# Second attention with q computed transposed and the last dense stage in its block: a decoder of four stages on one core

## What is computed

```python
x = x + tanh(g_xattn[0]) * attention0(layernorm(x), ctx)
x = x + tanh(g_ffn[0])   * swiglu(layernorm(x))
x = x + tanh(g_xattn[1]) * attention1(layernorm(x), ctx)
x = x + tanh(g_ffn[1])   * dense1(layernorm(x))

def attention1(latents, context):      # 32 heads, 8 key/value heads, head size 128
    kv = concatenate([context, latents], axis=1)          # 64 + 256 keys
    q = rms_norm((latents @ Wq).reshape(b, n, 32, 128), q_norm_w)
    k = rms_norm((kv @ Wk).reshape(b, m, 8, 128), k_norm_w)
    v = (kv @ Wv).reshape(b, m, 8, 128)
    p = softmax(q @ k.T / sqrt(128))
    return (p @ v) @ Wo

def dense1(x):                         # 1024 tokens
    base, logits = x @ base_W.T, x @ gate_W.T             # 28 experts
    gate_full = scatter of softmax(top2(logits))          # two of 28
    h = (x @ lora_A) * (gate_full * 2)                    # 28 x rank 8
    return base + h @ lora_B
```

## Time and profile before

| | us |
|---|---|
| median of 3 runs | 1496.01 |
| lowest and highest | 1492.74 to 1496.33 |
| profiled execution, its own time | 1493.15 |
| its span in the trace | 1491.4 |
| PE busy | 1399.5 (94%) |
| DVE busy | 1058.6 (71%) |
| ACT busy | 798.0 (54%) |

### The profile page before, as it was taken

One profiled execution on the slowest core, in us unless ns is written; L12 is line 12 of the kernel. 1 busy time (PEld: TensorE's weight loads), 2 busy tenths in 40 slices (PEclk: granted clock), 3 DMA queues, 4 the chain that ended last, 5 costly groups with the idle time before them and its releaser, 6 DMA issues. The chain is left out here.

```text
span 1491.4 us, 24301 instructions
## 1 busy us (share of the span) xinstructions
PE 1399.5 (94%) x7976; PEld 1199.3 (80%) x7976; DVE 1058.6 (71%) x2794; ACT 798.0 (54%) x2204; POOL 462.6 (31%) x588
## 2 busy tenths in 40 slices
PE   4999999998999998999999999999999999999889
PEld 4888888887778876888878888888888878887767
DVE  6777777778633337787787787787787777787765
ACT  4777777775211315565555555555555555555521
POOL 3855555554954612111111121111211111112120
PEclk8999999999999999999999999999999999999989
DMA  4111122111321301001001001001001000100001
GB/s 191 71 55 60 70 70 70 65 61 44 104 68 43 123 1 71 1 1 72 1 1 71 0 1 71 0 1 71 0 1 71 0 36 35 38 18 1 1 0 57
DMA packets 14958, 63.96 MB, mean 43 GB/s; under 512 B 1760, under 2 KB 1760, under 8 KB 10656
## 3 DMA queue, kind: packets, MB, share of 16 engines
q1 hardware_dynamic: 14880, 63.07, 11.8%
HBM read 60.97 MB, written 2.10 MB: 42 GB/s over the span
## 5 line engine op out<-in xcount | busy, mean ns | idle before, releaser
L1251 ACT ACTIVATE p<-psum,nb,rq 128x320 f32<-128x320 f32 x256 | 155.3, 614 | 161.8 <-DVE nb L1034 161.8
L55 PE MATMUL psum<-w1q_hi,xnT_lo 128*128 128x512 f32 x256 | 107.2, 419 | 12.8 <-DVE v_lo L1054 8.3
L964 POOL TENSOR_TENSOR rk<-ssk,rms_eps 128x3 f32<-128x3 f32 x32 | 6.3, 196 | 349.9 <-DVE ssk L1071 349.9
L999 DVE TENSOR_TENSOR pT_lo<-psum,pT_hi 128x512 fp32r<-128x512 f32 x128 | 88.1, 689 | 32.5 <-ACT pT_hi L1174 30.7
L1030 DVE TENSOR_REDUCE mx<-psum 128x2 f32<-128x640 f32 x128 | 105.0, 820 | 5.7
L1215 ACT ACTIVATE q_raw<-psum 128x512 f32<-128x512 f32 x64 | 38.3, 598 | 121.3 <-PE psum L57 121.3
L361 DVE TENSOR_TENSOR VW_lo<-psum,VW_hi 64x512 fp32r<-64x512 f32 x128 | 88.0, 688 | 19.1 <-ACT VW_hi L457 17.5
L57 PE MATMUL psum<-w1q_hi,xnT_hi 128*128 128x512 f32 x256 | 100.6, 393 | 0.0
L55 PE MATMUL psum<-w1o_hi,oT_lo 128*128 128x512 f32 x256 | 100.4, 392 | 0.0
L56 PE MATMUL psum<-w1o_lo,oT_hi 128*128 128x512 f32 x256 | 100.3, 392 | 0.0
L56 PE MATMUL psum<-w1q_lo,xnT_hi 128*128 128x512 f32 x256 | 99.8, 390 | 0.0
(11 more groups left out here) (245 smaller groups left out, 4676.8 us busy)
## 6 DMA issues: line engine op xcount, KB each, us to landing
raw_q<-in_w0q SPq DMA_DIRECT2D x8, 1024.0 KB, 4.8
raw_o<-in_w0o SPq DMA_DIRECT2D x8, 1024.0 KB, 4.8
raw_q<-in_w1q SPq DMA_DIRECT2D x8, 1024.0 KB, 7.5
raw_o<-in_w1o SPq DMA_DIRECT2D x8, 1024.0 KB, 4.8
raw_kv<-in_w_gu SPq DMA_DIRECT2D x10, 512.0 KB, 3.6
raw_gu<-in_w_gu SPq DMA_DIRECT2D x10, 512.0 KB, 3.6
raw_kv<-in_w0kv SPq DMA_DIRECT2D x8, 515.0 KB, 3.3
raw_kv<-in_w1kv SPq DMA_DIRECT2D x8, 512.0 KB, 5.5
```

The source lines that it names most:

```text
L55: pe.matmul(out, w[1], m[0], start=start, stop=False)
L999: last = dve.tensor_tensor(k.pT[1][:, kt, 2 * hp:2 * hp + 2, :], bank.rearrange("p (h q) -> p h q", h=2), f(k.pT[0][:, kt, 2 * hp:2 * hp + ...
L1251: last = act.activation(k.p1[:, tile, h, :], s_pair(j)[:, h % 2, :], ACT.Exp, bias=k.nb[:, i:i + 1], scale=k.rq[:, i:i + 1], accum_out=k.r ...
```

## The change

Attention 1. q is made transposed: the weights are the stationary operand and the normed tokens stream, so that a bank holds two heads x 256 tokens, channels on the partitions. A half is 24 products of 256 columns instead of 12 of 512. ACT makes `qT_hi` from it (`q_hi`), DVE `qT_lo` (`q_lo`), then ACT squares it into `q_sq` (`q_square`). The sum over channels, which now lie on the partitions, is made by PE: eight products with `q_sq` stationary (128x128, plain float32) and a column of ones streaming, each into one column of a bank. DVE adds epsilon and copies it to `ssq`. `q_raw`, its copies, the squares on DVE and the transpositions of q go. `PAIRS` runs by head pair, so that a head pair's rows are complete after two of four scores.

Last dense stage. The block `ffn1_phase` becomes a class whose steps are called from attention 1's `tail`, with the turns and outputs of unit 31 between them. Its weights are split in unit 31 in place of the next g's (`split_next = b == BATCH - 1`), those of `w_b` by POOL, the buffers are views of attention 1's (`w_q`, `qT`, `kT`, `q_sq`, `dump`), and `ag` has one bank instead of two.

```diff
-    PAIRS = [(0, 0), (0, 1), (1, 0), (1, 1)]
+    PAIRS = [(0, 0), (1, 0), (0, 1), (1, 1)]
...
-            def q_squares(n, b, tile):
-                dve.wait_ge(q_copied, 2 * n + tile + 1)
-                for h in range(GH):
...
+            def q_lo(n, b, hp):
+                dve.wait_ge(qt_hi, 2 * n + hp + 1)
+                dve.tensor_tensor(k.qT[1][:, 2 * hp:2 * hp + 2, :],
+                                  y_bank(b, "q", hp)[:, :].rearrange("p (h q) -> p h q", h=2),
+                                  f(k.qT[0][:, 2 * hp:2 * hp + 2, :]), ALU.subtract).then_inc(qt_split, 1)
...
                     if prev:
                         t_lo(n, b, 1)
+                    q_lo(n, b, 0)
                     dve.wait_ge(rk_ready, n + 1)
...
-                    q_squares(n, b, 0)
+                    q_lo(n, b, 1)
                     if prev:
                         t_lo(n, b, 4)
                         t_lo(n, b, 5)
-                    q_squares(n, b, 1)
-                    if prev:
                         pv_lo(n, b, 0)
+                    dve.wait_ge(ssq_full, n + 1)
+                    dve.tensor_scalar(k.ssq[:, :], x_bank(b, "ssq")[:, 0:2 * GH], HD * RMS_EPS, None,
+                                      ALU.add).then_inc(ssq_ready, 1)
                     dve.wait_ge(kt_hi, n + 1)
...
+            def q_hi(n, b, hp):
+                act.wait_ge(q_full, 2 * n + hp + 1)
+                act.activation(k.qT[0][:, 2 * hp:2 * hp + 2, :],
+                               y_bank(b, "q", hp)[:, :].rearrange("p (h q) -> p h q", h=2), ACT.Copy).then_inc(qt_hi, 1)
+
+            def q_square(n, b, hp):
+                act.wait_ge(qt_split, 2 * n + hp + 1)
+                act.activation(k.q_sq[:, hp, :], y_bank(b, "q", hp)[:, :], ACT.Square).then_inc(q_squared, 1)
...
                         if j in (1, 3):
-                            act.wait_ge(q_full, 2 * n + j // 2 + 1)
-                            act.activation(k.q_raw[:, j // 2, :], y_bank(b, "q", j // 2)[:, :], ACT.Copy)\
-                               .then_inc(q_copied, 1)
+                            if j == 3:
+                                q_square(n, b, 0)
+                            q_hi(n, b, j // 2)
+                    q_square(n, b, 1)
+                    if prev:
+                        pv_evac(n, b, 0)
...
-                        for c in range(CH):
-                            if prev and tile == 0 and c == CH - 1:
-                                pe.wait_ge(t_split, 6 * (n - 1) + 1)
-                            last = mm3(pe, y_bank(b, "q", tile)[:, :], [w[:, c, t * PART:(t + 1) * PART] for w in k.xnT],
-                                       [w[:, c, :] for w in k.w_q], c == 0, c == CH - 1)
+                        for hh in range(2):
+                            h = 2 * hp + hh
+                            for c in range(CH):
+                                if prev and hp == 0 and hh == 1 and c == CH - 1:
+                                    pe.wait_ge(t_split, 6 * (n - 1) + 1)
+                                last = mm3(pe, bank[:, hh * SEQ:(hh + 1) * SEQ],
+                                           [w[:, c, h * HD:(h + 1) * HD] for w in k.w_q],
+                                           [w[:, c, b * SEQ:(b + 1) * SEQ] for w in k.xnT], c == 0, c == CH - 1)
...
-                        for h in range(GH):
-                            last = pe.transpose(x_bank(b, "q", tile)[:, h * PART:(h + 1) * PART],
-                                                k.q_raw[:, tile, h * HD:(h + 1) * HD], k.ident[:, :])
+                    pe.wait_ge(q_squared, 2 * n + 2)
+                    for j, (tile, hp) in enumerate(PAIRS):
+                        for hh in range(2):
+                            at = hh * SEQ + tile * PART
+                            last = pe.matmul(x_bank(b, "ssq")[:, 2 * j + hh:2 * j + hh + 1], k.q_sq[:, hp, at:at + PART],
+                                             k.one[:, :], start=True, stop=True)
+                    last.then_inc(ssq_full, 1)
+                    if prev:
+                        p_v(n, b, 1)
...
+                ffn1.pe_ag(pe, 0)
+                turn(n, 0, 0, alone=True)
+                turn(n, 0, 1, alone=True)
+                ffn1.pe_ag(pe, 1)
+                ffn1.pe_base(pe, 0)
+                turn(n, 0, 2, alone=True)
+                turn(n, 0, 3, alone=True)
+                ffn1.pe_base(pe, 1)
+                turn(n, 0, 4, alone=True)
+                turn(n, 0, 5, alone=True)
+                pe.wait_ge(x_added, 2 * (n - 1))
+                p_v(n, 0, 0, alone=True)
+                ffn1.pe_ag(pe, 2)
                 p_v(n, 0, 1, alone=True)
+                ffn1.pe_base(pe, 2)
+                ffn1.pe_hgT(pe, 0)
+                out(n, 0, 0)
+                ffn1.pe_low_rank(pe, 0)
```

More of the change, by code:

```diff
@@ L18 @@
+import math
 import concourse.bass as bass
@@ L930, in piece, with weights @@
         return slice(i * n, (i + 1) * n)
+    def weights(kind, g, i):
+        s = piece(kind, i)
+        if kind == "kv" and isinstance(g, int) and g == NKV:
+            c = slice(2 * i, 2 * i + 2)
+            return k.raw_ag[:, c, :], k.w_ag[0][:, c, 0:LR + NEXP], k.w_ag[1][:, c, 0:LR + NEXP]
+        return raw[kind][:, s], flat[kind][0][:, s], flat[kind][1][:, s]
     def loop(eng, body, tail):
@@ L938, in loop @@
         tail(NKV * BATCH)
+    ffn1 = Ffn1(k, sem, ln, free={"kv": kv_wlo, "q": q_wlo, "exp": exp_done, "scores": s_full, "w_kv": kv_full,
+                                  "turned": t_split, "x": x_added, "whi": kv_whi}, conv=CONV, units=UNITS)
     with nc.Block() as block:
@@ L1105, in body @@
                     last.then_inc(kt_split, 1)
[L1106 to L1113, removed]
+                    if prev:
+                        pv_lo(n, b, 1)
+                    split_next = b == BATCH - 1
                     row_max(n, 0)
@@ L1226, in body @@
                         w_hi("q", g + 1, 0)
-                    for tile in range(2):
-                        act.wait_ge(qt_full, 2 * n + tile + 1)
-                        act.activation(k.qT[0][:, tile, :, :],
-                                       x_bank(b, "q", tile)[:, :].rearrange("p (h q) -> p h q", h=GH),
-                                       ACT.Copy).then_inc(qt_hi, 1)
-                        if prev and tile == 0:
-                            pv_evac(n, b, 1)
-                        if tile == 0:
-                            for late in ln_tiles(n):
-                                ln.act_norm(act, *late)
+                    if prev:
+                        pv_evac(n, b, 1)
+                    for late in ln_tiles(n):
+                        ln.act_norm(act, *late)
                     if split_next:
@@ L1624, in build, with ffn1_views, cut, twice @@
-def build(nc, d, out, phases=("attn0", "ffn0", "attn1", "ffn1")):
+    k.ffn1_load = load
+def ffn1_views(k):
+    k.raw_ag = k.raw_kv[:, 0:CH * (LR + NEXP)].rearrange("p (c n) -> p c n", c=CH)
+    k.w_ag = [w[:, :].rearrange("p (c n) -> p c n", c=CH) for w in k.w_kv]
+    k.w_base = k.w_q
+    k.w_b = [w[:, :, :].rearrange("p (t h) q -> p t (h q)", t=2) for w in k.qT]
+    spare = k.kT[0][:, :, :].rearrange("p b n -> p (b n)")
+    k.hgT = [spare[:, i * 512:(i + 1) * 512].rearrange("p (u c n) -> p u c n", u=2, c=2) for i in range(2)]
+    k.ag, k.hg = k.q_sq[:, :, 0:256], k.q_sq[:, :, 256:256 + LR]
+    small = k.dump[:, :, :].rearrange("p a b -> p (a b)")
+    at = [0]
+    def cut(n, dtype=None):
+        ap = small[:, at[0]:at[0] + n]
+        at[0] += 16 * math.ceil(n / 16)
+        return ap.bitcast(dtype) if dtype else ap
+    def twice(n, dtype=None):
+        return [cut(n, dtype) for _ in range(2)]
+    k.iota_i, k.iota = cut(NEXP, mybir.dt.int32), cut(NEXP)
+    k.top, k.idx, k.idxf = twice(8), twice(8, mybir.dt.uint32), twice(2)
+    k.gap, k.eg, k.pr = twice(1), twice(1), twice(4)
+    k.ga, k.gb, k.gm = twice(NEXP), twice(NEXP), twice(NEXP)
@@ L1626, in build @@
+def build(nc, d, out):
     k = Kernel()
@@ L1686, in build @@
-        done = sem("out_done")
-        with nc.Block() as block:
-            @block.sync
-            def _(sp):
-                sp.dma_start(out.rearrange("(t p) c -> p t c", p=PART), k.x[:, :, :]).then_inc(done, 16)
-                sp.wait_ge(done, 16)
+        with ExitStack() as scope:
+            k.bo, k.gbo = sb(scope, "bo", [HID]), sb(scope, "gbo", [HID])
+            k.w_q, k.w_o = pair(scope, "w0q", [QW]), pair(scope, "w0o", [QW])
+            k.bias, k.q_last = sb(scope, "bias", [GH + 2]), sb(scope, "q_last", [GH])
+            k.kvT = pair(scope, "kvT0", [2, BATCH * CTX])
+            k.WK = pair(scope, "WK", [CH, BATCH, GH, CTX])
+            k.VW = pair(scope, "VW", [GH // 2, BATCH, HID])
+            k.p0 = sb(scope, "p0", [4, GH * CTX])
+            k.nb0, k.sum0 = (sb(scope, n, [2, GH]) for n in ("nb0", "sum0"))
+            k.rinv0 = sb(scope, "rinv0", [4, GH])
+            k.pT0 = pair(scope, "pT0", [2, 2 * PART])
```

(8 more changed lines are left out.)

543 lines of the change are left out of this document (263 added, 280 removed).

## The result

The changed kernel takes 1524.93 us (median of 5 runs, 1523.99 to 1535.39), the kernel before 1494.68 us (5 runs, 1491.33 to 1496.33): ratio 1.022, 95% interval 1.019 to 1.025. It is slower by 30 us. Forecast were 1512 us and a range of 1482 to 1554: the sign and the range hold, the point is 13 us too low.

The account below looks back on a forecast made before the run. PE's instructions and waits were taken to bound attention 1, waits between engines the tail. 1493.15 + 29.8 (PE's work) + 2 (waits) - 14 (tail), plus 1 for timed runs, gave 1512 us; range 1482 to 1554, own range 1497 to 1525.

Parts of the forecast that it names:

- The products: Eight one-column float32 products per unit on PE in attention 1, two weight loads each: +1.74 us a unit.
- The first rival: A one-column product is as cheap as a transposition, one load each; kernel not slower, 1484 us; chance 0.15.
- the third: Four weight loads per one-column product, 3.49 instead of 1.74 us a unit: 1568 us; chance 0.12.
- The second rival: Load and product don't overlap when the kind changes, 1.3 us more a unit, +41 us: 1553 us; chance 0.11.
- q's projection: q's products on PE in attention 1, two halves a unit from 2.75 to 2.87 us each: +0.24 us a unit.
- The transpositions: q's transpositions and the slow step behind them leave PE's program in attention 1: -1.05 us a unit.
- The tail: Behind the last scores, the last dense stage's work fills PE's idle time: -14 us, between -9 and -18.
- the fourth rival: The tail gives nothing because DVE's chain of subtractions and routing bounds it: 1526 us; chance 0.04.
- Waits of PE in attention 1: PE's waits for other engines in attention 1 change by +2 us in sum, between -8 and +8.
- `v_lo`'s waits: PE's waits for `v_lo` at the loop's start in attention 1, 8.3 us, were to stay.
- My +6 us for the last turn: Before the one-column products PE waits some 0.45 instead of 0.25 us a unit for the last turn's subtraction: +6 us.
- The checks: Signs in the profile after: `q_sq` rows and their time, round time, waits, tail length, and what would prove the forecast wrong.

Follow-up runs that it names:

- the two halves: Attention 1 of before with the merged tail: 1484.45 us, ratio 0.992; new attention 1 with the last stage in its own block: 1542.26 us, ratio 1.030.
- the 64-column kernel: The changed kernel with 64 equal columns of ones instead of one, one result read: 1502.64 us, ratio 1.005 to the kernel before.
- two rows of four: The changed kernel with four of the eight one-column products ahead of the second value product and four behind it: 1500.95 us, ratio 1.003.

## Why the prediction was right, and where it was not

**The products** were the main term, and their working held: two halves of the weights, each loaded once, at the pace of loads. 1.81 us was measured and 1.74 predicted, +2 us over 32 units. The first rival (a load per product) and the third (four) are refuted by sixteen records and 1.81 us. Of the rule that true float32 takes four passes, which the prediction took from the Trainium skill (FP8 and Floating Point Precision, TensorE Precision Notes), the trace shows two loads and two products in the records; what a record does inside can't be seen, and at one column its pace, 0.113 us, is near that of the loads in the earlier trace rows, 0.109. The Trainium skill, TensorE: Matmul & The Clock Gate (Part 2, LDWEIGHTS), gives a load the time of its columns at 1.2 GHz, by which I estimate 107 ns for 128; the sixteen records, at 113 ns each, are 6% above it.

**The second rival** (load and product don't overlap at a change of kind) is refuted: it asked for 1.3 us more a unit, some 3.0 us for the eight products, and 1.81 were measured.

**q's projection**: a half takes 1105.32 - 1102.36 = 2.96 us with its slow first step, less 0.08 it is 2.88, predicted 2.87.

```profile
1102.36 0.36 PE L57 MATMUL psum<-xnT_hi,w1q_lo 128*128 128x256 f32 x1
...
1105.32 0.38 PE L1347 MATMUL psum<-ident,p 128*128 128x128 f32 x2
```

**The transpositions**: the scores follow `p_v(1)` without the slow step, as taken.

**The tail**: -15.0 us in the traces, 11 and 17 us in the two halves, -14 predicted, and all inside -9 to -18. The wait for ACT's return of the single bank, 1.68 us, had been set at 1.5; the fourth rival (DVE is the bound, and the tail gives nothing) is refuted by the 15 us; PE waits 0.9 us for DVE in the whole of it.

**The step that failed first: "Waits of PE in attention 1".** I put down +2 us and wrote that `v_lo`'s waits stay, because "they lie at the loop's start, ahead of any step that changes". They went. What the change relieves is DVE in the units ahead of the loop's start. That this relief is the cause is shown from both sides: the kernel before without six sums loses the waits, and the 64-column kernel with eight sums put back has them again. How it works, by the pause of DVE that goes with them, is not shown. My +6 us for the last turn was too high as well: its waits and those for `q_sq` are 8.0 us where 3.7 were. Measured: -9.8 us by the sum of the waits in the profiled execution, -7.5 us in the 64-column kernel; my low end was -8. That term was 9 to 12 us too high.

**The step that was missing: the clock.** I read 1.00 in the earlier trace rows for attention 1 and carried it over, though the earlier trace rows has 0.80 for the tail of before, where PE does little. That PE may lose its clock while it is busy without a gap was not in my sum or my rivals. It costs 34 us in the profiled execution and 22 to 24 us by the medians (64 columns, and two rows of four). Clock +22 to +24, waits -9 to -12, work +3 and the tail -1 come to +12 to +17, and 13 was measured. The forecast's point owes its nearness to the two misses being opposite; its sign doesn't: with the clock given back the kernel is still 0.3 and 0.5% slower in those two kernels, with intervals of 0.2 to 0.5 and 0.3 to 0.6%.

**The checks** named in advance: sixteen records, yes. 1.7 us, 1.81. A round of four units 109 us: 1223.33 - 1112.38 = 110.95 us with one stretch of 1.55 us in it, 109.4 without. Waits for `q_sq` and the last turn "about 14 us": 8.0. Last scores to the end 64 us: 66.7, at full clock. "I am wrong if DVE's relief empties waits that I left standing": it did.

## What to carry to other kernels

A product with few columns costs its weight loads, so count records of the type used: a float32 product has two, a float32r product or a float32 transposition one. Don't put many of them in one row: break the row with wide products, or widen it (64 columns cost nothing here, and took 19 of 22 stretches away), and look at the granted clock in windows of 2 us behind it, since windows of many units hide it. And when work leaves an engine that is "not the bound", sum the waits that this engine ends anywhere, also a unit later or at a loop's start, and look at its own pauses there, before calling the relief worthless.

## What the runs showed of the hardware that was not expected

- The granted clock falls to 1.2 GHz for some 2 to 4 us behind a row of sixteen one-column records (1.81 us), with PE busy all the time and 0 to 0.6 us idle before it. It does so behind 20 of the 32 rows. The Trainium skill (TensorE: Matmul & The Clock Gate, Why this matters for your kernels) advises against gaps without work between bursts; here the products themselves, back to back, are enough, and no gap is needed.
- With rows of eight such records (0.80 to 0.91 us), in float32 or in float32r, and with sixteen records of 64 columns, attention 1 has 1 to 3 such stretches, all beside waits of PE of 1.2 to 2.1 us. The kernel with the attention 1 of before and no such row also has 3, beside waits of 1.1 to 2.0 us; the kernel before, with waits as long, has none. Where eight sums a unit are put back on DVE, 4 of the 9 stretches follow a row of 64 columns.
- Which units are hit isn't told by the rows: those of 885.71 and 1112.38 us are alike, with the same 0.56 us of idle time before them, and one is hit. Why runs of one kernel differ in their count (0.968 to 0.977 mean clock) stays open too.
- 64 columns of float32 cost as much as one: 1.80 and 1.81 us for eight products.
- DVE pauses 2.3 us at five of the loop's rounds in the kernel before, with no wait shown, and not at all there when it has 1.28 us less work a unit.
